# Attention and FP4 feed-forward: GpSimd sums all key tiles, ScalarE copies the first columns, two heads in one bank, TensorE's order in a pair laid anew

## The chip, the cores and the metric

One core of one Trainium2 chip. The metric is the device time of one execution in microseconds; the kernel before took 3739.86 us, the median of 3 runs (3735.11 to 3740.07).

## The reference

The input x is (8, 1024, 512). It is normalised over its last axis, and the output is x plus two branches of the normalised rows: causal attention with 16 heads of 32, and a feed-forward whose weights and activations are quantised block by block to FP4 values.

```
qkv = x @ W_attn + b_attn                       # 512 -> 1536
att = einsum('bhqd,bhkd->bhqk', q, k) * 32 ** -0.5
att = where(causal, att, -inf); att = softmax(att)
y = einsum('bhqk,bhkd->bhqd', att, v); y @ W_proj + b_proj
gate, up = fp4_linear(xn, w_gate), fp4_linear(xn, w_up)   # 512 -> 1408
fp4_linear(silu(gate) * up, w_down)
x = x + attention + feed_forward
```

The change touches only the attention.

## The kernel before, in words

The attention runs first, batch by batch, then the feed-forward over 64 tiles of 128 rows. A batch is the projections (queries, keys, values; split into high and low 32-bit parts), then 8 pairs of heads, then the output projection. Engines run side by side, each with its own program in order, and wait for each other by counting semaphores.

In a pair the scores are made twice. First with queries on the partitions: 16 tiles (`T` steps; `scores` L1020, for two heads and eight tiles of 128 queries), masked by a bf16 product (`MT`; L1046); VectorE takes each row's maximum (`row_max` L649). Tiles go by turns to ps_s and to ps_dense bank 0. These tiles are those of the next pair, 13 of the 16 ahead of the step `MAX`, the other 3 behind it for the pair after. `MAX` (L1049) transposes the maxima, VectorE splits them into high and low parts (`split_max` L656), and SP moves them by two DMAs into two extra rows of the next pair's stack (`maxima` L445). Second with keys on the partitions: for each of the eight key tiles kt 0 to 7, from query kt * 128 on, in up to 4 parts (`S0` to `S3`; `transposed_scores` L1062), the maximum subtracted by the extra rows, the diagonal masked (`M`; L1077). The parts go in a ring of three banks, ps_st; ScalarE reads each with Exp into pt, or for kt 5 to 7 into `tail` (part of rob) (L933). kt 4 takes the space of kt 1. A pair before has 24 parts: 4 each for kt 0 to 3, 2 each for kt 4 to 7.

`P0` to `P7` (`times_v` L1082) multiply the exponentials with the values. The two heads and the even and odd query tiles go to four column groups of 32 of the array. They are plain 32-bit products, two instructions each in the trace; P3, P5, P6 and P7 of a pair run at the start of the next one. `DEN` (`denominators` L1097) sums the exponentials over the keys by a product with ones, for the pair before. GpSimd has summed kt 0 to 4 in SBUF first (`sum_up` L572, into stage): kt 0 + kt 1 for queries 128 on (L583), a copy of the first 128 queries by a multiplication with ones (L580), then kt 2, 3, 4 (L585). TensorE multiplies these sums and, each for itself, kt 5, 6 and 7. In the last pair of a batch GpSimd sums kt 0 to 2 only.

VectorE copies the denominators out of the bank (`copy_den` L664), SP spreads them over 64 partitions by four DMAs (`den_rows` L488), VectorE takes reciprocals (`INV`), SP writes them out and reads them back, and VectorE divides (`Y0`, `Y1`; L690) two pairs later. The next tile in ps_dense behind DEN waits for the copy (L1035).

STEPS (L96) writes TensorE's order in a pair by hand, one string for each key tile; VECTOR_STEPS (L106) VectorE's order (`R` a row maximum). EARLY and AFTER_DEN count T steps from STEPS; DEN waits until the tiles ahead of it that use its bank have been reduced (L1101). SP's queue within a pair is: den_rows of the pair before, its inverse, the next pair's maxima, the inverse's spread, and the loads of the pair four later once this pair's exponentials are done (L507 to L525). ScalarE waits at kt 5 for den_full of the pair before (L925), since DEN reads `tail`.

Of the kernel before, what the change touches and what calls it, by code (L numbers as in the profile page):

```python
# [44 lines left out]
def attention(nc, ctx, banks, memory, shared, x, w_attn, b_attn, w_proj, b_proj, w_gate, w_up, w_down, qk_scratch, ones_scratch,  # L45
# [20 lines left out]
    PARTS = [[(h, max(c * QC, kt * P), (c + 1) * QC - max(c * QC, kt * P))  # L66
              for c in reversed(range(NQ)) if (c + 1) * QC > kt * P for h in range(2)] for kt in range(ST)]
# [13 lines left out]
    def summed(p):  # L81

        return RINGED if p < PAIRS - 1 else 3


    SUM_ORDER = [1, 0, 2, 3, 4]
    FREED = {0: 2, 1: 1, 2: 3, 3: 4, 4: 5}
    SUMS = sum(summed(p) for p in range(PAIRS))
# [7 lines left out]
    STEPS = ["T T MT P3 P5 T MT S0 S1 T S2 S3 M2 MT M3 P6 DEN P7",  # L96
# [7 lines left out]


    VECTOR_STEPS = "R R R Y0 R Y1 DEN R R R R R R R INV R R MAX R R R"  # L106
# [3 lines left out]
    AHEAD_OF_ALL = EARLY + FLAT[:FLAT.index("S0")].count("T")  # L110
# [26 lines left out]
    assert ND % 2 == 0 and (PAIRS * NPARTS) % ST_RING == 0  # L137
# [17 lines left out]
    def sem(name):  # L155
# [73 lines left out]
    summed_up = sem("a_summed_up")  # L229
# [19 lines left out]
              v_done, *stack_in, s_full, s_max, m_full, m_hi, m_lo, m_in, st_full, st_exp, pv_done, summed_up, den_full,  # L249
# [26 lines left out]
    def sums(h):  # L276
        return stage[:, h].rearrange("p a n -> p (a n)")

# [90 lines left out]
    assert len(TWOS) * 2 == TILES and AHEAD_OF_ALL == 6  # L369
# [168 lines left out]
    def gpsimd(pool):  # L538
# [25 lines left out]
        def body(b, final):  # L564
            for t in range(XR, ST):
                inv_std(b, t)

            def x_and_bias(t):
                pool.wait_ge(res_in[t % 2], ONE + b * (ST // 2) * DMA + (t // 2 + 1) * DMA)
                nc.gpsimd.tensor_tensor(res[:, t % 2], res[:, t % 2], bp[:, :], ALU.add).then_inc(o_res, 1)  # L570

            def sum_up(p, kt):  # L572

                pool.wait_ge(st_exp, ONE + b * PAIRS * NPARTS + p * NPARTS + PART0[kt + 1])
                if kt > 1:
                    pool.wait_ge(summed_up, ONE + b * SUMS + p * RINGED + kt)
                both = stage[:, :, :, :].rearrange("p h a n -> p h (a n)")
                cols = slice(kt * P, S)
                if kt == 0:
                    nc.gpsimd.tensor_tensor(both[:, :, 0:P], exps(0)[:, :, 0:P], ones[:, 0:1].unsqueeze(2).to_broadcast([P, 2, P]),  # L580
                                            ALU.mult).then_inc(summed_up, 1)
                elif kt == 1:
                    nc.gpsimd.tensor_tensor(both[:, :, cols], exps(0)[:, :, cols], exps(1), ALU.add).then_inc(summed_up, 1)  # L583
                else:
                    nc.gpsimd.tensor_tensor(both[:, :, cols], both[:, :, cols], exps(kt), ALU.add).then_inc(summed_up, 1)  # L585

            for i in range(2):
                pool.wait_ge(qk_out[i], ONE + b * (NQK // 2) * DMA + (NQK // 2) * DMA)
            for p in range(PAIRS):
                if p == PAIRS - 1 and not final:  # L590
                    inv_std(b + 1, 0, XR)
                if p:
                    pool.wait_ge(den_full, ONE + b * PAIRS + p)
                for kt in SUM_ORDER[:summed(p)]:
                    sum_up(p, kt)
            pool.wait_ge(bias_sum, 1)
            for t in range(ST):
                x_and_bias(t)
# [249 lines left out]
    def scalar(act):  # L848
# [14 lines left out]
        def body(b, final, rest):  # L863
# [50 lines left out]
            for p in range(PAIRS):  # L914
                for kt in range(ST):
                    if kt == RINGED - 1:
                        act.wait_ge(pv_done, ONE + b * PAIRS * ST + p * ST + PV_AT[1] + 1)
                        act.wait_ge(summed_up, ONE + b * SUMS + p * RINGED + FREED[1])
                    elif kt < RINGED and p:
                        last = RINGED - 1 if kt == 1 else kt  # L920
                        act.wait_ge(pv_done, ONE + b * PAIRS * ST + (p - 1) * ST + PV_AT[last] + 1)
                        act.wait_ge(summed_up, ONE + b * SUMS + (p - 1) * RINGED + FREED[last])
                    if kt == RINGED:
                        if p:
                            act.wait_ge(den_full, ONE + b * PAIRS + p)  # L925
                            act.wait_ge(pv_done, ONE + b * PAIRS * ST + p * ST)
                        else:
                            act.wait_ge(o_sum, ONE + b * ST)
                            act.wait_ge(o_out[1], ONE + b * (ST // 2) * DMA)
                    for i, (h, q, n) in enumerate(PARTS[kt]):  # L930
                        w = p * NPARTS + PART0[kt] + i
                        act.wait_ge(st_full, ONE + b * PAIRS * NPARTS + w + 1)
                        nc.scalar.activation(exps(kt)[:, h, q - kt * P:q - kt * P + n], ps_st[:, w % ST_RING, 0:n], ACT.Exp,  # L933
                                             scale=SCALE).then_inc(st_exp, 1)
                    if final and kt == PIECE_AT[p]:
                        shared.load_gate_up(act, p)
# [31 lines left out]
    def tensor(pe):  # L968
# [20 lines left out]
        def body(b, final):  # L989
# [72 lines left out]
            def transposed_scores(p, kt, i):  # L1062
                h, q, n = PARTS[kt][i]
# [3 lines left out]
                if w == ST_RING - 1:  # L1067
# [4 lines left out]
                last = nc.tensor.matmul(ps_st[:, w % ST_RING, 0:n], stack(p)[0:KM, 2 + h, kt * P:(kt + 1) * P],  # L1072
                                        stack(p)[0:KM, h, q:q + n], start=True, stop=not diagonal)
# [3 lines left out]
            def mask_transposed(p, kt, i):  # L1077
                w = p * NPARTS + PART0[kt] + i
                nc.tensor.matmul(ps_st[:, w % ST_RING, 0:P], causal[:, :], identb[:, :], start=False,  # L1079
                                 stop=True).then_inc(st_full, 1)  # L1080
# [16 lines left out]
            def denominators(p):  # L1097
                pe.wait_ge(summed_up, ONE + b * SUMS + p * RINGED + summed(p))
# [3 lines left out]
                for kt in range(summed(p) - 1, ST):  # L1102
                    for s in range(2):
                        if parity_tiles(kt, s) >= ST:
                            continue
                        for h in range(2):
                            if kt < summed(p):
                                src, cols = by_tile(sums(h))[:, s::2], slice(0, QC)
                            else:
                                src, cols = exps_of_parity(kt, h, s), y_cols(kt, s)  # L1110
                            last = nc.tensor.matmul(by_tile(den_bank(p)[y_rows(h, s), cols]), ones[:, :], src,  # L1111
                                                    start=kt < summed(p), stop=kt == ST - 2 + s)
# [533 lines left out]
```

## Time and profile before

| | us |
|---|---|
| median of 3 runs | 3739.86 |
| lowest, highest | 3735.11, 3740.07 |
| profiled execution, its own time | 3740.65 |
| its span | 3738.8 |
| TensorE busy | 3660.0 (98%) |
| VectorE busy | 2638.5 (71%) |
| ScalarE busy | 1199.3 (32%) |
| GpSimd busy | 930.6 (25%) |

The attention takes the first 2,150 us or so, where GpSimd is at work; the rest is the feed-forward. In the page's 40 slices of the span TensorE is at nine tenths or more in all but the first.

### The profile page before, as it was taken

The numbers are of one execution on the slowest core, as the hardware profiler recorded it, in microseconds if no ns is written. First come the engines' busy times: TensorE is split into PE (matmuls) and PEld (weight loads), VectorE is DVE, ScalarE is ACT, GpSimd is POOL, SyncE is SP. The second block draws the span as 40 slices with busy tenths as digits, with TensorE's granted clock in tenths as the row PEclk, the third lists the DMA queues.
The fourth block names the chain that finished last, engine by engine and source line by source line (L and its number), as shares of the span: only waits on it lengthen the run. The fifth ranks groups of instructions, "written<-read, shape, count | busy, mean of one in ns | idle before, by whom it ended". The sixth has DMA issues, their size and how long they took to land.

```text
span 3738.8 us, 63849 instructions
## 1 busy us (share of the span) xinstructions
PE 3660.0 (98%) x21836; PEld 2699.9 (72%) x21836; DVE 2638.5 (71%) x3834; ACT 1199.3 (32%) x2313; POOL 930.6 (25%) x462
## 2 busy tenths in 40 slices
PE   8999999999999999999999999999999999999999
PEld 6657657657656566566565578888888888888887
DVE  6675766766766766766766667777777777777776
ACT  2542532533523524514414412222222222222222
POOL 0560741642632724615615500000000000000000
PEclk9999999999999999999999999999999999999999
DMA  6525435335336245254256331100111110011110
GB/s 199 124 72 178 109 101 175 77 123 165 80 120 173 63 144 155 58 185 123 73 179 172 119 122 34 34 31 28 34 34 34 34 32 31 30 34 34 34 34 28
DMA packets 180526, 337.02 MB, mean 90 GB/s; under 512 B 42688, under 2 KB 50368, under 8 KB 179392
## 3 DMA queue, kind: packets, MB, share of 16 engines
q1 hardware_dynamic: 156096, 280.47, 26.5%
q10 hardware_dynamic: 24192, 53.49, 4.2%
q8 instruction: 135, 2.21, 0.3%
q14 instruction: 103, 0.84, 0.1%
HBM read 213.92 MB, written 118.43 MB: 89 GB/s over the span
## 4 chain that ended last, share of the span: by engine, by line
PE 90%; issue 2%; DMA 2%; DVE 2%; POOL 2%; ACT 1%; SPq 0%; ACTq 0%; DVEq 0%; POOLq 0%
PE f_ps L1523 26%; PE ps_dense L1016 13%; PE f_ps_o L1535 13%; PE ps_st L1072 9%; PE ps_s L1041 5%; PE ps_y L1093 4%; PE ps_dense L1180 4%; PE ps_dense L1093 3%; PE ps_dense L1111 3%; PE ps_dense L1041 2%; PE f_ps L1515 1%; PE ps_st L1079 1%; DMA stack<-mr 1%; POOL stage L585 1%; PE ps_s L1046 1%
## 5 line engine op out<-in xcount | busy, mean ns | idle before, releaser
L1523 PE MATMUL f_ps<-wgu,xqt 128*128 128x512 f32 (+1 forms) x4608 | 992.9, 373 | 1.4 <-DVE xqt L1383 1.4
L1523 PEld LDWEIGHTS f_ps<-wgu,xqt 128*128 128x128 f32 x4608 | 842.4, 188 | 123.0 <-DVE xqt L1383 1.7
L933 ACT ACTIVATE pt<-ps_st 128x512 f32<-128x512 f32 (+3 forms) x1152 | 550.4, 526 | 540.4 <-PE ps_st L1072 354.8
L653 DVE TENSOR_REDUCE mx<-ps_s 128x1 f32<-128x640 f32 (+3 forms) x512 | 523.8, 1023 | 212.2 <-PE ps_s L1046 203.1
L585 POOL TENSOR_TENSOR stage<-stage,pt 128x1536 f32<-128x1536 f32 (+2 forms) x176 | 519.1, 2950 | 15.2
L1535 PE MATMUL f_ps_o<-wd,hqt 128*128 128x512 f32 x2112 | 513.4, 396 | 0.2 <-DVE hqt L1409 0.2
L583 POOL TENSOR_TENSOR stage<-pt 128x1792 f32<-128x1792 f32 x64 | 256.5, 4009 | 882.6 <-ACT pt L933 882.6
L1535 PEld LDWEIGHTS f_ps_o<-wd,hqt 128*128 128x128 f32 x2112 | 392.6, 189 | 79.5 <-DVE hqt L1409 0.6
L1016 PE MATMUL ps_dense<-arena,wa 128*128 128x512 f32 x1536 | 384.1, 399 | 11.1 <-DVE rob L701 6.2
L1016 PEld LDWEIGHTS ps_dense<-arena,wa 128*128 128x128 f32 x1536 | 281.1, 189 | 73.7 <-issue 10.8
L653 DVE TENSOR_REDUCE mx<-ps_dense 128x1 f32<-128x128 f32 (+3 forms) x424 | 204.4, 482 | 87.5 <-PE ps_dense L1046 78.1
L1072 PE MATMUL ps_st<-stack 98*128 98x512 f32 (+3 forms) x768 | 250.1, 389 | 16.3 <-DMA stack<-mr 13.7
L1072 PE MATMUL ps_st<-arena 98*128 98x512 f32 (+3 forms) x768 | 252.4, 394 | 8.5 <-ACT pt L933 6.8
L1180 PE MATMUL ps_dense<-wp,yt 128*128 128x512 f32 x512 | 227.1, 594 | 2.1 <-DVE rob L701 2.0
L1072 PEld LDWEIGHTS ps_st<-arena 98*128 98x128 f32 x768 | 131.8, 189 | 133.3 <-ACT pt L933 101.0
L1470 ACT ACTIVATE silu<-f_ps 128x512 f32<-128x512 f32 (+1 forms) x192 | 106.8, 556 | 367.7 <-PE f_ps L1523 367.7
L1072 PEld LDWEIGHTS ps_st<-stack 98*128 98x128 f32 x768 | 132.4, 190 | 127.6 <-ACT pt L933 87.1
L899 ACT ACTIVATE stage<-ps_dense,bqk 128x512 fp32r<-128x512 f32 x128 | 87.6, 687 | 365.4 <-PE ps_dense L1016 310.0
L1465 ACT ACTIVATE ha<-ht 128x1408 f32<-128x1408 f32 x63 | 87.0, 1381 | 326.6 <-DVE ht L1306 326.6
L1402 DVE TENSOR_TENSOR h<-silu,f_ps 128x512 f32<-128x512 f32 (+1 forms) x192 | 122.6, 639 | 94.1 <-ACT silu L1470 90.6
L1016 PE MATMUL ps_dense<-wa,arena 128*128 128x512 f32 x768 | 188.1, 395 | 0.0
L1079 PE MATMUL ps_st<-identb,causal 128*128 128x128 bf16 x1024 | 183.1, 224 | 0.0
(135 smaller groups left out, 4943.1 us busy)
## 6 DMA issues: line engine op xcount, KB each, us to landing
qk_scratch<-stage SPq DMA_DIRECT2D x128, 512.0 KB, 2.8
stack<-qk_scratch SPq DMA_DIRECT2D x192, 256.0 KB
arena<-qk_scratch SPq DMA_DIRECT2D x192, 256.0 KB
xs<-in_L_attn_x SPq DMA_DIRECT2D x64, 256.0 KB, 3.6
rob<-in_L_attn_x ACTq DMA_DIRECT2D x64, 256.0 KB, 2.8
acc_scratch<-rob ACTq DMA_DIRECT2D x64, 256.0 KB, 2.2
xt<-in_L_attn_x SPq DMA_DIRECT2D x64, 256.0 KB, 2.6
at<-acc_scratch SPq DMA_DIRECT2D x64, 256.0 KB, 2.6
```

Of the source, the lines that this page charges most:

```text
L583: nc.gpsimd.tensor_tensor(both[:, :, cols], exps(0)[:, :, cols], exps(1), ALU.add).then_inc(summed_up, 1)
L585: nc.gpsimd.tensor_tensor(both[:, :, cols], both[:, :, cols], exps(kt), ALU.add).then_inc(summed_up, 1)
L653: nc.vector.tensor_reduce(mx[:, h * ST + q:h * ST + q + 1], scores_bank(p, n)[:, 0:(q + 1) * P], axis=AX.X, op=ALU.max, negate=True).then_ ...
L933: nc.scalar.activation(exps(kt)[:, h, q - kt * P:q - kt * P + n], ps_st[:, w % ST_RING, 0:n], ACT.Exp, scale=SCALE).then_inc(st_exp, 1)
L1016: last = nc.tensor.matmul(bank(*use), left(lh, k), right(rh, k), start=n == 0, stop=n == len(terms) - 1)
L1041: nc.tensor.matmul(out[:, k0:k1], qs, stack(p)[0:KS, 2 + h, k0:k1], start=True, stop=k1 < keys)
L1072: last = nc.tensor.matmul(ps_st[:, w % ST_RING, 0:n], stack(p)[0:KM, 2 + h, kt * P:(kt + 1) * P], stack(p)[0:KM, h, q:q + n], start=True, ...
L1079: nc.tensor.matmul(ps_st[:, w % ST_RING, 0:P], causal[:, :], identb[:, :], start=False, stop=True).then_inc(st_full, 1)
L1093: last = nc.tensor.matmul(by_tile(y_bank(p)[y_rows(h, s), y_cols(kt, s)]), v_head(kt, p, h), exps_of_parity(kt, h, s), start=kt == 0, stop ...
L1180: last = nc.tensor.matmul(bank("P", k), yt[:, g, t * P:(t + 1) * P], wp[:, g, :], start=g == 0, stop=g == G - 1)
L1523: last = nc.tensor.matmul(ps[:, SLOT[c], gu, 0:n].rearrange("p (j n) -> p j n", n=P), xqt[:, a, k], wgu[:, b, gu * FC + f // P:gu * FC + ( ...
L1535: last = nc.tensor.matmul(ps_o[:, :], hqt[:, a, k], wd[:, b, k], start=i == 0, stop=i == len(terms) - 1)
```

## The change

In all pairs but a batch's last GpSimd sums all eight key tiles (seven additions, kt 1 to 7); DEN is then the four products of the sums alone. The first 128 queries of kt 0 are copied into stage by ScalarE, ahead of the exponentials of kt 5, with a semaphore of its own (first_sums) for which DEN waits. For kt 6 and 7 both heads' scores go to one bank, with one mask product and one exponential; a pair has 22 parts. STEPS and VECTOR_STEPS are written anew: DEN moves from the end of the first string to the third, P3 and P5 behind the pair's first scores, MAX to the end of the fourth, and T tiles are mostly masked one by one. AHEAD_OF_ALL stays 6. Hunks that only name the semaphore or loosen an assertion, and blank lines, are left out.

```diff
@@ -63,8 +63,11 @@
-    PARTS = [[(h, max(c * QC, kt * P), (c + 1) * QC - max(c * QC, kt * P))
-              for c in reversed(range(NQ)) if (c + 1) * QC > kt * P for h in range(2)] for kt in range(ST)]
+    PAIRED = 6
+    PARTS = [[(range(h, h + 1), max(c * QC, kt * P), (c + 1) * QC - max(c * QC, kt * P))
+              for c in reversed(range(NQ)) if (c + 1) * QC > kt * P for h in range(2)] for kt in range(PAIRED)]
+    PARTS += [[(range(2), kt * P, (ST - kt) * P)] for kt in range(PAIRED, ST)]
     NPARTS = sum(len(parts) for parts in PARTS)
     PART0 = [sum(len(parts) for parts in PARTS[:kt]) for kt in range(ST + 1)]
     ST_RING, SLOTS, XR = 3, 4, 4
@@ -80,12 +83,13 @@
     def summed(p):
-        return RINGED if p < PAIRS - 1 else 3
-    SUM_ORDER = [1, 0, 2, 3, 4]
-    FREED = {0: 2, 1: 1, 2: 3, 3: 4, 4: 5}
-    SUMS = sum(summed(p) for p in range(PAIRS))
+        return ST if p < PAIRS - 1 else 3
+    SUM_ORDER = [*range(1, ST)]
+    FREED = {0: 1, 1: 1, 2: 2, 3: 3, 4: 4}
+    SUMS = sum(summed(p) - 1 for p in range(PAIRS))
     TILES = 2 * ST
     TILE = [(h, q) for h in range(2) for t in range(ST // 2) for q in (ST // 2 + t, ST // 2 - 1 - t)]
@@ -93,21 +97,22 @@
-    STEPS = ["T T MT P3 P5 T MT S0 S1 T S2 S3 M2 MT M3 P6 DEN P7",
-             "S0 S1 S2 T MT T MT M2 T S3 MT M3",
-             "S0 S1 T S2 T MT M2 P0 S3 T T MT M3 P1",
-             "S0 T T MT S1 S2 S3 M2 P2",
-             "S0 M3- M0 MAX T S1 MT M1",
-             "S0 T S1 M0 MT M1",
-             "S0 T MT M0 P4 S1",
-             "S0 S1 M1- M0 M1"]
-    VECTOR_STEPS = "R R R Y0 R Y1 DEN R R R R R R R INV R R MAX R R R"
+    STEPS = ["T MT T MT S0 S1 T P3 MT T MT S2 S3 T MT M2 M3",
+             "S0 P5 T MT T MT S1 S2 S3 M2 M3 T MT",
+             "S0 DEN P6 P7 P0 S1 T MT S2 S3 T MT M2 M3 T MT P1 T T MT",
+             "S0 S1 P2 S2 M2 S3 M3 MAX",
+             "S0 T MT M0 S1 M1",
+             "S0 T M0 MT S1 T MT M1",
+             "S0 P4 M0",
+             "S0 M0"]
+    VECTOR_STEPS = "R R R R R R R Y0 Y1 DEN R R R R R R INV MAX R R R"
     FLAT = " ".join(STEPS).split()
     EARLY = TILES - FLAT[:FLAT.index("MAX")].count("T")
-    AHEAD_OF_ALL = EARLY + FLAT[:FLAT.index("S0")].count("T")
+    AHEAD_OF_ALL = 6
     AFTER_DEN = EARLY + FLAT[:FLAT.index("DEN")].count("T")
     PV_HERE = [int(step[1:]) for u in range(ST) for step in STEPS[u].split() if step[0] == "P" and int(step[1:]) < u]
@@ -275,6 +280,9 @@
     def sums(h):
         return stage[:, h].rearrange("p a n -> p (a n)")
+    def both_sums():
+        return stage[:, :, :, :].rearrange("p h a n -> p h (a n)")
     def by_tile(a):
         return a.rearrange("p (t n) -> p t n", n=P)
@@ -573,13 +581,10 @@
                 pool.wait_ge(st_exp, ONE + b * PAIRS * NPARTS + p * NPARTS + PART0[kt + 1])
                 if kt > 1:
-                    pool.wait_ge(summed_up, ONE + b * SUMS + p * RINGED + kt)
-                both = stage[:, :, :, :].rearrange("p h a n -> p h (a n)")
+                    pool.wait_ge(summed_up, ONE + b * SUMS + p * (ST - 1) + kt - 1)
+                both = both_sums()
                 cols = slice(kt * P, S)
-                if kt == 0:
-                    nc.gpsimd.tensor_tensor(both[:, :, 0:P], exps(0)[:, :, 0:P], ones[:, 0:1].unsqueeze(2).to_broadcast([P, 2, P]),
-                                            ALU.mult).then_inc(summed_up, 1)
-                elif kt == 1:
+                if kt == 1:
                     nc.gpsimd.tensor_tensor(both[:, :, cols], exps(0)[:, :, cols], exps(1), ALU.add).then_inc(summed_up, 1)
                 else:
                     nc.gpsimd.tensor_tensor(both[:, :, cols], both[:, :, cols], exps(kt), ALU.add).then_inc(summed_up, 1)
@@ -591,7 +596,7 @@
                     inv_std(b + 1, 0, XR)
                 if p:
                     pool.wait_ge(den_full, ONE + b * PAIRS + p)
-                for kt in SUM_ORDER[:summed(p)]:
+                for kt in SUM_ORDER[:summed(p) - 1]:
                     sum_up(p, kt)
             pool.wait_ge(bias_sum, 1)
             for t in range(ST):
@@ -915,11 +920,11 @@
                 for kt in range(ST):
                     if kt == RINGED - 1:
                         act.wait_ge(pv_done, ONE + b * PAIRS * ST + p * ST + PV_AT[1] + 1)
-                        act.wait_ge(summed_up, ONE + b * SUMS + p * RINGED + FREED[1])
+                        act.wait_ge(summed_up, ONE + b * SUMS + p * (ST - 1) + FREED[1])
                     elif kt < RINGED and p:
                         last = RINGED - 1 if kt == 1 else kt
                         act.wait_ge(pv_done, ONE + b * PAIRS * ST + (p - 1) * ST + PV_AT[last] + 1)
-                        act.wait_ge(summed_up, ONE + b * SUMS + (p - 1) * RINGED + FREED[last])
+                        act.wait_ge(summed_up, ONE + b * SUMS + (p - 1) * (ST - 1) + FREED[last])
                     if kt == RINGED:
                         if p:
                             act.wait_ge(den_full, ONE + b * PAIRS + p)
@@ -927,11 +932,18 @@
                         else:
                             act.wait_ge(o_sum, ONE + b * ST)
                             act.wait_ge(o_out[1], ONE + b * (ST // 2) * DMA)
-                    for i, (h, q, n) in enumerate(PARTS[kt]):
+                            for i in range(2):
+                                act.wait_ge(qk_out[i], ONE + b * (NQK // 2) * DMA + (NQK // 2) * DMA)
+                        nc.scalar.activation(both_sums()[:, :, 0:P], exps(0)[:, :, 0:P], ACT.Copy).then_inc(first_sums, 1)
+                    for i, (heads, q, n) in enumerate(PARTS[kt]):
                         w = p * NPARTS + PART0[kt] + i
                         act.wait_ge(st_full, ONE + b * PAIRS * NPARTS + w + 1)
-                        nc.scalar.activation(exps(kt)[:, h, q - kt * P:q - kt * P + n], ps_st[:, w % ST_RING, 0:n], ACT.Exp,
-                                             scale=SCALE).then_inc(st_exp, 1)
+                        if len(heads) == 1:
+                            nc.scalar.activation(exps(kt)[:, heads[0], q - kt * P:q - kt * P + n], ps_st[:, w % ST_RING, 0:n],
+                                                 ACT.Exp, scale=SCALE).then_inc(st_exp, 1)
+                        else:
+                            nc.scalar.activation(exps(kt), ps_st[:, w % ST_RING, 0:2 * n].rearrange("p (h n) -> p h n", h=2),
+                                                 ACT.Exp, scale=SCALE).then_inc(st_exp, 1)
                     if final and kt == PIECE_AT[p]:
                         shared.load_gate_up(act, p)
@@ -1060,7 +1072,7 @@
                 last.then_inc(q_full, 1)
             def transposed_scores(p, kt, i):
-                h, q, n = PARTS[kt][i]
+                heads, q, n = PARTS[kt][i]
                 w = p * NPARTS + PART0[kt] + i
                 if (kt, i) == (0, 0):
                     pe.wait_ge(m_in, ONE + b * PAIRS * 2 * DMA + (p + 1) * 2 * DMA)
@@ -1069,15 +1081,21 @@
                     pe.wait_ge(s_max, ONE + b * PAIRS * TILES + TILES + AHEAD_OF_ALL)
                 pe.wait_ge(st_exp, ONE + b * PAIRS * NPARTS + max(w - ST_RING + 1, 0))
                 diagonal = q == kt * P
-                last = nc.tensor.matmul(ps_st[:, w % ST_RING, 0:n], stack(p)[0:KM, 2 + h, kt * P:(kt + 1) * P],
-                                        stack(p)[0:KM, h, q:q + n], start=True, stop=not diagonal)
+                for j, h in enumerate(heads):
+                    last = nc.tensor.matmul(ps_st[:, w % ST_RING, j * n:(j + 1) * n], stack(p)[0:KM, 2 + h, kt * P:(kt + 1) * P],
+                                            stack(p)[0:KM, h, q:q + n], start=j == 0, stop=not diagonal)
                 if not diagonal:
                     last.then_inc(st_full, 1)
             def mask_transposed(p, kt, i):
+                heads, _, n = PARTS[kt][i]
                 w = p * NPARTS + PART0[kt] + i
-                nc.tensor.matmul(ps_st[:, w % ST_RING, 0:P], causal[:, :], identb[:, :], start=False,
-                                 stop=True).then_inc(st_full, 1)
+                if len(heads) == 1:
+                    nc.tensor.matmul(ps_st[:, w % ST_RING, 0:P], causal[:, :], identb[:, :], start=False,
+                                     stop=True).then_inc(st_full, 1)
+                else:
+                    nc.tensor.matmul(ps_st[:, w % ST_RING, 0:2 * n].rearrange("p (h n) -> p h n", h=2)[:, :, 0:P], causal[:, :],
+                                     identb[:, :].unsqueeze(1).to_broadcast([P, 2, P]), start=False, stop=True).then_inc(st_full, 1)
             def times_v(p, kt):
@@ -1095,21 +1113,22 @@
                 last.then_inc(pv_done, 1)
             def denominators(p):
-                pe.wait_ge(summed_up, ONE + b * SUMS + p * RINGED + summed(p))
+                pe.wait_ge(summed_up, ONE + b * SUMS + p * (ST - 1) + summed(p) - 1)
+                pe.wait_ge(first_sums, ONE + b * PAIRS + p + 1)
                 if p + 2 < PAIRS:
                     pe.wait_ge(s_max, ONE + b * PAIRS * TILES + (p + 2) * TILES + AFTER_DEN // 2 * 2)
-                for kt in range(summed(p) - 1, ST):
+                for s in range(2):
+                    for h in range(2):
+                        last = nc.tensor.matmul(by_tile(den_bank(p)[y_rows(h, s)]), ones[:, :], by_tile(sums(h))[:, s::2],
+                                                start=True, stop=summed(p) == ST)
+                for kt in range(summed(p), ST):
                     for s in range(2):
                         if parity_tiles(kt, s) >= ST:
                             continue
                         for h in range(2):
-                            if kt < summed(p):
-                                src, cols = by_tile(sums(h))[:, s::2], slice(0, QC)
-                            else:
-                                src, cols = exps_of_parity(kt, h, s), y_cols(kt, s)
-                            last = nc.tensor.matmul(by_tile(den_bank(p)[y_rows(h, s), cols]), ones[:, :], src,
-                                                    start=kt < summed(p), stop=kt == ST - 2 + s)
+                            last = nc.tensor.matmul(by_tile(den_bank(p)[y_rows(h, s), y_cols(kt, s)]), ones[:, :],
+                                                    exps_of_parity(kt, h, s), start=False, stop=kt == ST - 2 + s)
                 last.then_inc(den_full, 1)
             split = 0
```

## Rows read from the trace of the kernel before

**Rows 1.** The chain that ended last: share of the span by engine and line.
```profile
PE 90%; issue 2%; DMA 2%; DVE 2%; POOL 2%; ACT 1%; SPq 0%; ACTq 0%; DVEq 0%; POOLq 0%
PE f_ps L1523 26%; PE ps_dense L1016 13%; PE f_ps_o L1535 13%; PE ps_st L1072 9%; PE ps_s L1041 5%; PE ps_y L1093 4%; PE ps_dense L1180 4%; PE ps_dense L1093 3%; PE ps_dense L1111 3%; PE ps_dense L1041 2%; PE f_ps L1515 1%; PE ps_st L1079 1%; DMA stack<-mr 1%; POOL stage L585 1%; PE ps_s L1046 1%
```

**Rows 2.** Busy time of each engine (instructions) in one pair, then granted clock and DMA.
```profile
722.10:741.70 19.60, 19.60 (x171) 12.04 (x170) 14.53 (x23) 10.60 (x25) 13.36 (x5) 1.00 0.11 26
```

**Rows 3.** TensorE in order of time, pairs 4 and 5: start, us, instructions.
```profile
715.13 0.70 PE L1072 MATMUL ps_st<-stack 98*128 98x512 f32 x2
...
717.15 1.04 PE L1111 MATMUL ps_dense<-stage,ones 128*32 128x512 f32 x8
...
725.83 0.50 PE L1072 MATMUL ps_st<-stack 98*128 98x512 f32 x1
...
726.17 0.63 PE L1041 MATMUL ps_s<-stack 96*128 96x512 f32 x2
...
730.38 0.22 PE L1079 MATMUL ps_st<-identb,causal 128*128 128x128 bf16 x1
...
730.41 0.36 PE L1072 MATMUL ps_st<-stack 98*128 98x256 f32 x1
...
730.61 0.56 PE L1041 MATMUL ps_s<-arena 96*128 96x512 f32 x2
...
736.74 1.04 PE L1111 MATMUL ps_dense<-stage,ones 128*32 128x512 f32 x8
...
737.60 1.05 PE L1111 MATMUL ps_dense<-rob,ones 128*32 128x128 f32 x20
...
738.48 0.39 PE L1093 MATMUL ps_dense<-rob,v 128*32 128x128 f32 x4
```

**Rows 4.** TensorE in order of time, the last pair of the same batch.
```profile
774.92 1.07 PE L1111 MATMUL ps_dense<-stage,ones 128*32 128x512 f32 x8 [0.47 <-POOL stage L585]
...
789.33 0.62 PE L1111 MATMUL ps_s<-stage,ones 128*32 128x512 f32 x2
...
792.65 1.53 PE L976 MATMUL ps_st<-ident,xs 128*128 128x128 f32 x12
```

**Rows 5.** Groups by line and shape, GpSimd in the attention: busy us, mean ns.
```profile
L585 POOL TENSOR_TENSOR stage<-stage,pt 128x1536 f32<-128x1536 f32 x64 | 222.6, 3478 | 5.5
...
L585 POOL TENSOR_TENSOR stage<-stage,pt 128x1280 f32<-128x1280 f32 x56 | 163.8, 2926 | 4.8
...
L585 POOL TENSOR_TENSOR stage<-stage,pt 128x1024 f32<-128x1024 f32 x56 | 132.7, 2370 | 4.8
```

**Rows 6.** GpSimd in order of time, two pairs.
```profile
726.78 8.94 POOL L585 TENSOR_TENSOR stage<-stage,pt 128x1536 f32<-128x1536 f32 x3
...
741.71 4.01 POOL L583 TENSOR_TENSOR stage<-pt 128x1792 f32<-128x1792 f32 x1 [5.99 <-ACT pt L933]
```

**Rows 7.** VectorE: three lines' durations (ns min/median/max), then its order of time.
```profile
L670 DVE COPY rob<-ps_dense x56: 691/692/694, 126.2 to 2120.9; 128x512 f32<-128x512 f32 x56
...
L615 DVE TENSOR_SCALAR xs<-xs,mv x56: 533/542/3684, 247.2 to 1904.1; 128x512 f32<-128x512 f32 x56
...
L659 DVE CAST mr<-ps_dense x56: 278/279/280, 115.3 to 2111.8; 16x128 fp32r<-16x128 f32 x56
...
776.97 0.69 DVE L670 COPY rob<-ps_dense 128x512 f32<-128x512 f32 x1 [1.78 <-PE ps_dense L1111]
...
783.05 0.25 DVE L674 RECIPROCAL inv<-den 128x16 f32<-128x16 f32 x1 [5.39 <-DMA den<-rob]
```

**Rows 8.** Start of a batch's second pair: TensorE's waits, its order of time, granted clock.
```profile
PE ps_st L1072 <- DMA stack<-mr: 13.7, 8, 4.7
...
654.86 0.86 PE L1072 MATMUL ps_st<-stack 98*128 98x512 f32 x2 [1.71 <-DMA stack<-mr]
...
658.13 1.33 PE L1111 MATMUL ps_dense<-stage,ones 128*32 128x512 f32 x8
...
657.00:658.00 1.00, 1.00 (x13) 0.56 (x15) 0.30 (x1) 0.41 (x1) 0.00 (x0) 0.50 1.08 221
```

More of the change, by code:

```diff
@@ L136, in attention @@
     assert NQ == 2 and XR == PER and AHEAD == ST - XR and len(QK) == NQK and len(PROJ) == NQK + ST + ST - XR
-    assert ND % 2 == 0 and (PAIRS * NPARTS) % ST_RING == 0
+    assert ND % 2 == 0
     F = w_gate.shape[0]
@@ L228, in attention @@
     bias_cols, bias_full, bias_sum = sem("a_bias_cols"), sem("a_bias_full"), sem("a_bias_sum")
-    summed_up = sem("a_summed_up")
+    summed_up, first_sums = sem("a_summed_up"), sem("a_first_sums")
     den_full = sem("a_den_full")
@@ L248, in attention @@
     LOOPED = [*x_in, bn_part, bn_tile, var_eps, rstd, normed, kept, d_full, t_full, t_hi, t_lo, qk_hi, qk_lo, *qk_out,
-              v_done, *stack_in, s_full, s_max, m_full, m_hi, m_lo, m_in, st_full, st_exp, pv_done, summed_up, den_full,
+              v_done, *stack_in, s_full, s_max, m_full, m_hi, m_lo, m_in, st_full, st_exp, pv_done, summed_up, first_sums, den_full,
               den_copy, den_in, inverted, last_inverted, inv_out, inv_in, y_div, *res_in, o_res, o_sum, *o_out,
@@ L368, in attention @@
         BESIDE[at] = [(1, 2 * i), (1, 2 * i + 1)]
-    assert len(TWOS) * 2 == TILES and AHEAD_OF_ALL == 6
+    assert len(TWOS) * 2 == TILES and AHEAD_OF_ALL >= EARLY + FLAT[:FLAT.index("S0")].count("T")
     NEEDS = {("QK", i): (c + 1) * PER for i, (_, _, c) in enumerate(QK)}
```

## The prediction

> **What bounds the kernel now.** I read the chain of waits first: TensorE holds 90% of it, and about 30% of the whole sits on the attention's lines (ps_st, ps_s, ps_y, ps_dense of L1041 to L1111) [rows 1]. So only what TensorE does or waits for counts. One steady pair by windows: TensorE is busy for all of its 19.6 us, VectorE 14.5, ScalarE 10.6, GpSimd 13.4 [rows 2]. The two DEN steps of rows 3 stand 736.74 - 717.15 = 19.59 us apart: that is the period of a pair, and TensorE's own work sets it.
>
> I cut a batch at its DEN steps (the order number is that of the pair whose denominators they make): A, from pair 1's first key scores to DEN(0); B, the five intervals DEN(0) to DEN(5); C, DEN(5) to DEN(6); D, DEN(6) to the end of DEN(7). Before, B's interval is 19.59; C is 774.92 - (736.74 + 19.59) = 18.59; D is 792.65 - 774.92 = 17.7 [rows 3, 4]. What comes ahead of A and behind D is the same code.
>
> **B, the steady pair.** Each term is a difference on TensorE.
> - DEN: its 20 instructions on the last three key tiles take 738.48 - 737.60 = 0.88 us [rows 3], and go. The eight on the sums stay, 0.86 us.
> - Masks: T and S tiles are masked at once now, one by one. In the old order a 32-bit product comes straight behind a mask 9 times in a pair, in the new one 20 times (counted in STEPS). Such a return costs an unhidden weight load: from the mask at 730.38 to the next scores at 730.61 are 0.23 us for 128 + 256 columns; at 0.42 ns a column (DEN: 4 x 512 columns, an estimate, in 0.86) that is 0.16, so 0.07 is left [rows 3]. 11 x 0.07 = +0.77. The bounds: 0, and the 0.13 that 512 columns have over their 0.21 behind a times-V step (725.83 to 726.17) [rows 3], so 0 to 1.4; I take the row of the same kind, a mask.
> - Leaving times-V steps: 6 exits into 32-bit products become 4, two go into a mask: about -0.1; five of the six times-V groups are now entered from a 32-bit product rather than a mask, no row of that; -0.5 to +0.2, I take -0.2. Fewer short products back to back: -0.15. One mask over two heads instead of two, twice a pair: -0.03.
> - Short waits in the old order (the tile behind DEN on VectorE's copy, two on its maxima), some 0.1 each: -0.3, if the new order has none.
> Sum: -0.88 + 0.77 - 0.1 - 0.2 - 0.15 - 0.03 - 0.3 = -0.9. Pair 18.7 us, B = -4.5 a batch.
>
> Does a wait come instead? GpSimd: sums of key tiles 1 to 4 take 4.01 [rows 6] + 3.48 + 2.93 + 2.37 [rows 5]; each 256 elements less are 0.53 to 0.56 less, so 5, 6, 7 take an estimated 1.81, 1.26, 0.70. With six gaps of 0.065 (three L585 as one block take 8.94 [rows 6] against 8.78 by the means) that is 16.95 us. It now runs DEN to DEN: the first sum waits for den_full, DEN for the last sum. 16.95 + 0.86 + 0.2 of entry + 0.17 of two releases (0.05 was seen behind POOL at 774.92) = 18.2. That is 0.5 us under 18.7: no wait, but the floor. Before, it ended its block at 735.72 and then sat 6.0 us until the exponentials of key tile 1 [rows 6].
> ScalarE: two exponentials saved, one copy of 256 columns added; with 10.6 of 19.6 busy [rows 2] both hide, at worst 0.4 us of it is seen. VectorE: before DEN it reduces seven tiles and divides twice; by laying the steps out with those durations I get the reduction that DEN needs 0.1 to 0.2 us ahead, the division that P0 needs 0.2 ahead: thin, up to +0.3 if they miss. The inverse chain: copy to reciprocal took 783.05 - 777.66 = 5.4 us where the DMA was waited for [rows 7]; copy to INV are six reductions, about 5.7 us, and behind INV on SP's queue stand the inverse's DMA, then the maxima's. Their landing has some 1.5 us to spare before the next pair's first key scores. In ahead of these there are 4.7 us of TensorE work from MAX instead of 6.2, as P3 and P5 stand behind them now.
>
> **A, the start.** Pair 1's first scores wait for the maxima's DMA, which lies behind pair 2's and 3's loads: 13.7 us over 8 batches, 4.7 the longest [rows 8]. The DMA lands when it did; TensorE is there 1.5 us sooner, so the hole grows from 1 to 1.7 us (most batches) to 2.5 to 3.2, and the work comes behind it. From the first scores to DEN were 717.15 - 715.13 = 2.0 us [rows 3]. Now there are 9 key-score products and 6 tiles (7,680 columns, 3.2 us), 10 masks (0.6), P3 and P5 (1.07 + 0.5 of entries and exits), 8 returns (0.6): 6.1. A = +4.1.
> **C.** Pair 6 has no tiles behind MAX, pair 7 none: TensorE would be at DEN(6) 15.5 us behind DEN(5) (2.0 + 10.6 for the rest of pair 6, less DEN's, and pair 7's nine key scores at ScalarE's speed), GpSimd's cycle says 18.2. C = 18.2 - 18.6 = -0.4, with a hole of about 2.6 us ahead of DEN(6).
> **D.** Kt 0 and 1 of pair 7 are ahead of DEN now. Behind DEN(6): DEN 1.05, P6 P7 0.43, P0 0.85, P1 and P2 2.0 with entries, key scores of tiles 2 to 7 with masks and returns 3.9, P4 0.65, P3 P5 P6 P7 1.8, DEN(7) as before 792.65 - 789.33 = 3.3 [rows 4], ring waits 0.3: 14.3. D = -3.4. VectorE's chain (copy, 5.4 of DMA, norms, divide) ends just then and has the projections' start for cover, as before.
> **The clock.** Behind the 1.71 us hole [rows 8] the granted clock was 0.50, the lower of its two levels; first scores to DEN took 658.13 - 654.86 = 3.3 instead of 2.0, and some 0.3 more was lost after. So a fall costs about 1.6 us. The other holes before are shorter, most near 1 to 1.5 us, and not each was followed by a fall (an estimate: two or three of eight). Two longer holes a batch: I count 1.4 falls more a batch, +2.2; bounds 0 and 3.2.
>
> **The sum.** A +4.1, B -4.5, C -0.4, D -3.4, clock +2.2: -2.0 us a batch, -16 for 8. The profiled execution took 3740.65 us (span 3738.8, 1.9 around it), 0.8 over the median of 3739.86 and no more than 0.6 over the highest: 3740.7 - 16 = 3725, against the median 3724.
>
> **A rule against the change.** SBUF — State Buffer, section "Who interferes with whom", of the Trainium skill: VectorE and GpSimd share a pair of ports under an exclusive lock; copies and tensor_scalar can want it, the loser waits for the other's whole instruction. Rows first: L615, a tensor_scalar SBUF to SBUF, has 542 ns as median and 3684 as its most, beside a GpSimd add of 3.5 us; L670, the copy of the denominators out of PSUM, has 691 to 694 in all 56, but GpSimd stood still by it; now its 4 us add starts at the same moment. The cast L659, also out of PSUM, has 278 to 280 always, and GpSimd ran beside it [rows 7]. The trace agrees with the rule for L615, and speaks against its reach to sources in PSUM.
>
> **Rivals.**
> 1. GpSimd becomes the bound: returns cost less than 0.03, and the pair stands at 18.2. For it: its cycle is just 0.5 below. Against: the count of returns. B = -6.9; 3724 - 19 = 3705, and 3688 if the clock never falls. Chance 0.2.
> 2. Slower: the alternation of masks and scores in u0 to u2 costs 0.13 or more a return, the upper row. The pair gains 0.25, B = -1.2, a batch +1.3 or more, and with three falls' worth of clock +2.3: 3750 (3745 to 3758). It decides once a pair gains under 0.5, from 0.11 a return: A's and the holes' +2.5 are then no longer paid. For it: 20 against 9. Against: the 0.07 measured behind masks. Chance 0.14.
> 3. Level: gain and holes cancel (a pair gains 0.4 to 0.6, or P0 and DEN wait their 0.3 for VectorE): 3738. Chance 0.2. TensorE: Matmul & The Clock Gate, section "LDWEIGHTS", of the Trainium skill puts a load of 128 columns at an estimated 107 ns; unhidden in all 11 new returns the pair would gain 0.5 and the time stay at 3740. The rows show 70 ns left over behind a mask, so I weigh it no more than that.
> 4. The copy waits for GpSimd's 4.0 us add [rows 6]: the tile behind DEN waits, less the 1.8 us of P6, P7, P0, S1 ahead of it: +2.9 a pair after its gain, in 56 pairs some 3870. Chance 0.02.
> 5. That it doesn't do what it says (exponentials of tiles 6 and 7 in two banks still): excluded by the code.
>
> **Chances.** The forecast has 0.44, 3724, with its own range of 3708 to 3736 (B by 0.3 us a pair either way, 12 us, and the clock). What a measurement of this kernel can tell is 0.2%, 7.5 us. Faster: 0.42 of the forecast and 0.2 of rival 1. Same: rival 3 and 0.02 of the forecast, less 0.02 of its edges: 0.21. Slower: 0.14 + 0.02, 0.01 more from rival 3's edge: 0.17. The range, 3690 to 3748, reaches to rival 1 and into rival 2.
>
> **What would show it.** DEN to DEN 18.7 us in pairs 1 to 5; at 18.2 with TensorE's L1111 waiting for POOL in each, rival 1; over 19.1, rival 2, by gaps behind masks. L1111 with 8 instructions a pair and none from rob, GpSimd with seven ops back to back. A hole ahead of pair 1's first scores of 2.5 to 3.2 us, one ahead of DEN(6) of 2 to 4, granted clock 0.5 behind both. DEN(6) to DEN(7)'s end 14.3 to 16. Wrong would be: no holes, a wait at P0 or at the tile behind DEN in each pair, L670 over 0.7 us.

## The result, and the profile after

The changed kernel took 3748.30 us (median of 20 runs, 3738.02 to 3759.94); the kernel before, 3739.87 (20 runs). The ratio is 1.0026, 95% interval 1.0018 to 1.0034: slower, by about 9 us, where 16 less was forecast. The profiled execution took 3741.61, one of its quickest.

Page of the changed kernel: span, TensorE's busy time, its granted clock by slices.
```profile
span 3739.8 us, 61509 instructions
...
PE 3629.0 (97%) x20588; PEld 2610.8 (70%) x20588; DVE 2618.2 (70%) x3834; ACT 1190.2 (32%) x2249; POOL 1109.5 (30%) x566
...
PEclk9999999999999999999999999999999999999999
```
TensorE is busy 31 us less than before in the same span. The slices are too coarse for the reason: the mean granted clock of the run is 0.987, before 0.996. In windows of 1 us through the attention I added up what is missing to 1.00: 8.5 us in 4 falls before, 42.6 us in 17 falls after. (A fall here is a stretch in which the granted clock is at 0.50; half of its length is lost clock.) The other runs agree: the quickest (3738.0) had a clock of 0.987, the slowest (3759.9) 0.981; 0.006 of 3,750 us are 22. The median run has 0.985.

A steady pair, windows as in [rows 2].
```profile
717.99:736.59 18.60, 18.60 (x150) 10.28 (x148) 14.29 (x23) 10.36 (x23) 16.62 (x8) 1.00 0.25 56
```
The pair takes 18.60 us; 18.7 was forecast. But not every pair does: DEN steps lie 18.61, 19.21, 18.63, 18.61 and 19.59 us apart in this batch.

TensorE's waits in the attention (us in total, times, longest), as in [rows 8].
```profile
PE ps_st L1085 <- DMA stack<-mr: 29.7, 8, 7.0
PE ps_dense L1123 <- POOL stage L590: 17.1, 8, 2.5
...
PE ps_st L1085 <- DMA arena<-mr: 6.6, 15, 0.9
```
The first row was 13.7, the second 3.8; the third is new: the waits for the maxima in pairs 3, 6 and 7.

The two holes of one batch on TensorE, answering to [rows 8] and [rows 4]: first key scores of pair 1, DEN(0); the last scores ahead of DEN(6), DEN(6), DEN(7).
```profile
654.37 1.22 PE L1085 MATMUL ps_st<-stack 98*128 98x512 f32 x2 [3.14 <-DMA stack<-mr]
...
663.12 1.07 PE L1123 MATMUL ps_dense<-stage,ones 128*32 128x512 f32 x8
...
773.63 0.50 PE L1085 MATMUL ps_st<-arena 98*128 98x512 f32 x1
776.16 1.93 PE L1123 MATMUL ps_dense<-stage,ones 128*32 128x512 f32 x8 [2.03 <-POOL stage L590]
...
787.89 0.62 PE L1123 MATMUL ps_s<-stage,ones 128*32 128x512 f32 x2
```
Their windows: us, TensorE busy, ..., granted clock (third from the end).
```profile
652.00:660.00 8.00, 5.63 (x22) 2.91 (x22) 2.20 (x4) 1.23 (x3) 5.16 (x4) 0.57 0.89 200
653.00:659.00 6.00, 4.63 (x17) 2.26 (x18) 0.84 (x2) 1.09 (x2) 4.16 (x4) 0.50 1.00 219
775.00:779.00 4.00, 2.83 (x24) 1.35 (x28) 0.69 (x1) 0.05 (x1) 2.93 (x5) 0.59 0.02 4
776.00:779.00 3.00, 2.83 (x24) 1.35 (x28) 0.69 (x1) 0.00 (x0) 2.01 (x4) 0.50 0.03 5
```
In this batch the holes have the length that was forecast (2.5 to 3.2, 2 to 4). Over all eight, the first is 2.7 to 3.5 us, 7.0 in the last batch, and the one ahead of DEN(6) 1.8 to 2.5. In this batch the clock then sits at 0.50, the lower level, for 6.8 us at the first hole and 3.4 at the second. DEN's eight instructions take 1.9 us at 776.16, against 1.07.

GpSimd, answering to [rows 6], and the copy of the denominators.
```profile
759.02 4.00 POOL L588 TENSOR_TENSOR stage<-pt 128x1792 f32<-128x1792 f32 x1 [2.47 <-PE ps_dense L1123]
763.10 8.95 POOL L590 TENSOR_TENSOR stage<-stage,pt 128x1536 f32<-128x1536 f32 x3
772.13 3.98 POOL L590 TENSOR_TENSOR stage<-stage,rob 128x768 f32<-128x768 f32 x3
```
```profile
L675 DVE COPY rob<-ps_dense x56: 690/692/693, 132.1 to 2123.6; 128x512 f32<-128x512 f32 x56
```
The three new sums take 3.98 us (3.77 was the estimate, without the gaps between them); the copy is not held up by the add beside it (rival 4 falls).

### The profile page after: what moved, and what is told of

It reads as the page before. It is cut to its first block, busy times and chain, and to the rows that moved or that the text cites. A ratio compares the mean times of both kernels' runs of the same rounds, so it can differ in the third digit from the quotient of the medians.

```text
span 3739.8 us, 61509 instructions
## 1 busy us (share of the span) xinstructions
PE 3629.0 (97%) x20588; PEld 2610.8 (70%) x20588; DVE 2618.2 (70%) x3834; ACT 1190.2 (32%) x2249; POOL 1109.5 (30%) x566
## 4 chain that ended last, share of the span: by engine, by line
PE 89%; DMA 3%; issue 3%; DVE 2%; POOL 1%; ACT 1%; SPq 1%; ACTq 0%; DVEq 0%; POOLq 0%
PE f_ps L1542 26%; PE ps_dense L1028 13%; PE f_ps_o L1554 13%; PE ps_st L1085 7%; PE ps_s L1053 5%; PE ps_dense L1199 5%; PE ps_y L1111 4%; PE ps_dense L1111 4%; PE ps_dense L1123 2%; PE ps_dense L1053 1%; DMA stack<-mr 1%; PE f_ps L1534 1%; DMA arena<-mr 1%; POOL stage L590 1%; PE ps_st L1094 1%
## 5 line engine op out<-in xcount | busy, mean ns | idle before, releaser
L942 ACT ACTIVATE pt<-ps_st 128x512 f32<-128x512 f32 (+3 forms) x1152 | 537.9, 526 | 570.2 <-PE ps_st L1085 398.8
L1085 PE MATMUL ps_st<-stack 98*128 98x512 f32 (+3 forms) x768 | 260.4, 405 | 30.0 <-DMA stack<-mr 29.7
L1085 PE MATMUL ps_st<-arena 98*128 98x512 f32 (+3 forms) x768 | 254.9, 402 | 10.2 <-DMA arena<-mr 6.6
L590 POOL TENSOR_TENSOR stage<-stage,rob 128x768 f32<-128x768 f32 x168 | 215.5, 1283 | 14.6
```

The source lines that it names most:

```text
L942: nc.scalar.activation(exps(kt)[:, heads[0], q - kt * P:q - kt * P + n], ps_st[:, w % ST_RING, 0:n], ACT.Exp, scale=SCALE).then_inc(st_exp, 1)
L1085: last = nc.tensor.matmul(ps_st[:, w % ST_RING, j * n:(j + 1) * n], stack(p)[0:KM, 2 + h, kt * P:(kt + 1) * P], stack(p)[0:KM, h, q:q + n] ...
```

## The experiments

Theory: the steps are worth about what was forecast, and the clock falls behind the two holes take it back. Times are medians, each with its ratio to the kernel before on the same chip; the changed kernel stands at 1.0026. The chips differ a little, so a difference between two versions can come out some 3 us apart by times and by ratios.

**e1: TensorE kept busy in both holes.**
```diff
+                    if p == 1:
+                        filler(12)      # 128x512 bf16 products into ps_y, ahead of the wait for m_in
...
+                if p == PAIRS - 2:
+                    pe.wait_ge(y_div, ONE + b * PAIRS * 2 + (PAIRS - 2) * 2)
+                    filler(9)           # ahead of the wait for summed_up
```


> The changed kernel with idle TensorE time filled: twelve bf16 products of 512 columns into a free bank ahead of the wait for the maxima in each batch's second pair, nine ahead of the wait for GpSimd at DEN(6). They change no value and shorten no wait. Theory (the clock falls behind the two longer holes are the term I mis-sized): granted clock back from 0.987 to about 0.995, one or two falls in the attention instead of 17, and 22 to 34 us less than the changed kernel, 3714 to 3726. Rival 1 (the falls are absorbed by later waits, the loss is in the order of the steps): within 4 us of the changed kernel. Rival 2 (fillers lengthen the holes): slower by up to 5 us.

3710.45, ratio 0.9919 (0.9906 to 0.9932): 38 us less than the changed kernel (40 by the ratios; 22 to 34 was expected), by work that does nothing. Two falls are left, both in the last batch, 8.5 us of lost clock. The batch from above:
```profile
644.65 2.75 PE L1076 MATMUL ps_y<-identb,causal 128*128 128x512 bf16 x12
648.14 0.73 PE L1092 MATMUL ps_st<-stack 98*128 98x512 f32 x2 [0.74 <-DMA stack<-mr]
...
654.53 1.06 PE L1133 MATMUL ps_dense<-stage,ones 128*32 128x512 f32 x8
...
766.59 1.07 PE L1133 MATMUL ps_dense<-stage,ones 128*32 128x512 f32 x8 [0.30 <-POOL stage L590]
...
776.89 0.62 PE L1133 MATMUL ps_s<-stage,ones 128*32 128x512 f32 x2
```
Scores to DEN(0) take 6.4 us instead of 8.75, DEN(6) to DEN(7) 10.3 instead of 11.7. The waits themselves are no shorter: 2.75 us of filler and 0.74 of idle time stand where 3.14 us of idle time stood. The theory stands.

**e12: the same filler in the kernel before** (five products, first hole only).

> The kernel before with five bf16 products of 512 columns ahead of the wait for the maxima in each batch's second pair, to have it without clock falls too. It had four falls in the attention, 8.5 us of lost clock, not all of it under work. Theory: 3732 to 3737, so that the change without the clock is worth 3710 against some 3735, and the clock is why it was not seen. Rival (fillers give more than the clock, as they also shift the work): under 3725.

3737.70, ratio 0.9998 (0.9989 to 1.0007): no difference. The run can't say what a fall costs, though: of the four falls before, this filler takes away two (1.7 us of lost clock each, near 655 and 1188 us), the two of the last batch stay, and its interval is 3 to 4 us wide on either side. What it gives is the comparison without the added falls: 3710 against 3738, 27 us (30 by the ratios). The forecast without its clock term is 4.2 us a batch, 34 us. So the steps are worth a little less than was forecast, and most of the miss is the clock.

**e2: pair 3's loads behind pair 1's maxima.**
```diff
-            later = stack_loads(2) + stack_loads(3)
+            later = stack_loads(2)
...
                     maxima(p + 1)
+                if p == 0:
+                    for args in stack_loads(3):
+                        load(*args)
```


> The changed kernel with the seven loads of pair 3's stack issued behind the maxima of pair 1 on SP's queue, not before pair 0. Theory (the maxima's DMA queues behind 3 MB of loads, so the hole ahead of pair 1's first scores is DMA backlog): the wait for stack<-mr falls from 29.7 us to under 12 us in total, no clock fall behind it, 20 to 30 us less than the changed kernel. Rival (the landing is set by when MAX comes, or by the loads of pair 4 issued behind): wait stays over 24 us, time within 5 us of the changed kernel.

3707.96, ratio 0.9911 (0.9897 to 0.9925), 40 us less (20 to 30 was expected). The wait for stack<-mr is gone. From issue to landing, the two DMAs of pair 1's maxima take, in the batch from above, in the changed kernel and then here:
```profile
DMA to landing us min/median/max: 5.1/5.6/6.2
DMA to landing us min/median/max: 1.8/1.8/1.8
```
So the first hole is a small DMA behind or beside the stack loads. Some comes back as waits for GpSimd and the split maxima (DEN(0) to DEN(1) 19.9 instead of 18.6, and 26.7 instead of 18.8 in the last batch); 11 falls are left, 7 of them at DEN(6).

**e6: the same edit in the kernel before.**

> The kernel before with the seven loads of pair 3's stack behind the maxima of pair 1. It had the hole ahead of pair 1's first scores too, but 1.3 us shorter, and four clock falls. Theory: stack<-mr waits 13.7 to under 5 us, 3724 to 3732. Rival (only the changed kernel's order suffers from these loads): 3737 to 3742.

A miss: 3764.18, ratio 1.0061 (1.0047 to 1.0074), slower by 22. VectorE in pair 1:
```profile
669.87 0.41 DVE L656 TENSOR_REDUCE mx<-ps_dense 128x1 f32<-128x256 f32 x1
673.51 0.25 DVE L677 RECIPROCAL inv<-den 128x16 f32<-128x16 f32 x1 [3.23 <-DMA den<-rob]
```
The loads now run beside the DMAs of the denominators. Those of pair 1 in this batch, from issue to landing, in the kernel before and then here:
```profile
DMA to landing us min/median/max: 1.7/1.7/1.7
DMA to landing us min/median/max: 7.2/7.7/7.9
```
INV waits for them in VectorE's order, ahead of the last maxima, and TensorE waits for those: DEN(0) to DEN(1) takes 21.5 to 30 us instead of 19.6 to 20.2. In the changed kernel DEN(0) comes some 4 us of work later, and the same DMAs take 5.2 us in e2. The same wait was only moved.

**e4: five of the eight sums in pair 6.**
```diff
-        return ST if p < PAIRS - 1 else 3
+        return ST if p < PAIRS - 2 else 5 if p == PAIRS - 2 else 3
```
(and running offsets for summed_up)

> The changed kernel with GpSimd summing only kt 1 to 4 of a batch's last-but-one pair; DEN(6) multiplies kt 5 to 7 itself, as before the change (0.88 us more TensorE work in 8 pairs). Theory (DEN(6) waits for GpSimd, 17.1 us in 8 batches, and the clock falls behind it): that wait goes to 0, no fall at the batch's end, 15 to 22 us less than the changed kernel. Rival (ScalarE or the inverse chain bounds the last pair anyway): the wait reappears within the last pair, 0 to 5 us.

3726.51, ratio 0.9963 (0.9949 to 0.9978): 22 us less. DEN(5) to DEN(6) takes 16.1 to 16.6 us instead of 18.4, no wait for GpSimd, no fall behind it.

**e5: e2 and e4 together.**

> The changed kernel with both holes shortened: pair 3's loads behind pair 1's maxima, and GpSimd summing only kt 1 to 4 of a batch's last-but-one pair. Theory (each hole costs its length and a clock fall behind it, the two are independent): 3708 less some 14 to 20 us: 3688 to 3696, under 5 falls in the attention. Rival (with one hole gone the other's cost moves on into a new wait for GpSimd or VectorE): 3700 to 3708.

3688.19, ratio 0.9859 (0.9844 to 0.9874): 52 us less than the kernel before, the best version here. The two repairs nearly add.

**e3: P3 and P5 ahead of the first key scores again.**
```diff
-    STEPS = ["T MT T MT S0 S1 T P3 MT T MT S2 S3 T MT M2 M3",
-             "S0 P5 T MT T MT S1 S2 S3 M2 M3 T MT",
+    STEPS = ["T MT P3 P5 T MT S0 S1 T MT T MT S2 S3 T MT M2 M3",
+             "S0 T MT T MT S1 S2 S3 M2 M3 T MT",
```


> The changed kernel with P3 and P5 put back ahead of the pair's first key scores; all else as it is. Theory (the hole grew because 1.2 us of work was moved behind the wait): stack<-mr waits fall from 29.7 by 8 x 1.2 us to about 20, the waits for arena<-mr in steady pairs (6.6 us) vanish, intervals of 19.1 to 19.6 us between DEN steps go to 18.6; 12 to 25 us less than the changed kernel, the larger figure if clock falls go with them. Rival (P3 and P5 ahead only shift the wait to the scores' ring or to VectorE): within 5 us.

A miss: 3766.37, ratio 1.0066 (1.0054 to 1.0078), 18 us slower. Its waits, same view as above:
```profile
PE ps_s L1053 <- DVE mx L658: 36.5, 88, 5.0
PE ps_st L1085 <- DMA stack<-mr: 19.3, 8, 5.7
```
The hole shrank as expected (29.7 to 19.3), but VectorE runs dry while P3 and P5 run, then tiles wait for it: 19.58 us in nearly every pair. VectorE in one of them:
```profile
724.42 1.09 DVE L658 TENSOR_REDUCE mx<-ps_s 128x1 f32<-128x896 f32 x1 [1.33 <-PE ps_s L1058]
```
The clock is worse too: 58 us lost in the attention of the profiled execution, where the changed kernel lost 42.6, although the holes are shorter. Ahead of pair 1's first scores they are 1.6 to 2.2 us in seven batches, and the falls behind them last 6.8 or 10.2 us. A shorter hole did not make a shorter fall.

**e9, e10: smaller moves of that kind, on e5** (P3 alone ahead; or a third tile ahead).

> The version with both holes shortened (3688), with P3 alone put ahead of the pair's first key scores (P5 stays behind). Pairs 3 and 6 still lose 0.6 us each to the wait for the maxima, and pair 7 some. Theory (0.8 us of cover ends that wait, and VectorE has enough tiles to bridge P3): 18.6 in all intervals from DEN(1) on, 3676 to 3684. Rival (as when P3 and P5 both went ahead: VectorE runs dry and tiles wait for it): 19 us or more in every pair, 3700 to 3730.

> The same version (3688) with three tiles ahead of the first key scores instead of two, P3 behind them. 0.17 us of cover, and VectorE is fed sooner. Theory: the wait in pairs 3 and 6 shrinks by 0.2 us, 3683 to 3688. Rival (the third tile waits for VectorE and delays the key scores, ScalarE starves): 3690 to 3710.

3704.34 (0.9908; 0.9893 to 0.9923) and 3694.57 (0.9883; 0.9868 to 0.9898), both slower than e5: 19.4 and 19.06 us in most pairs, where e5 has 18.6 in some and 19.2 in others. Both rivals were right.

**e11: masks together, on e1** ("T T MT" for "T MT T MT" in the first string, and behind P5).

> The filled changed kernel (3710) with two mask steps merged into the next: the first two tiles of a pair and the first two behind P5 are masked together, so that two returns of a 32-bit product behind a mask go. By my prediction's term that is 2 x 0.07 us in 56 pairs, 8 us less: 3701 to 3706. Rival (the first mask of the two comes 0.4 us later, and VectorE with its 0.8 us a tile waits for it, so tiles wait later): 3715 to 3740, VectorE's waits longer.

3725.30 (0.9967; 0.9955 to 0.9979), 15 us slower than e1 (18 by the ratios), where my term for returns gave 8 less. VectorE of e11:
```profile
729.40 0.56 DVE L658 TENSOR_REDUCE mx<-ps_dense 128x1 f32<-128x384 f32 x1 [1.12 <-PE ps_s L1058]
```
It starts that tile 1.12 us after its last work, in e1 0.72 after. The pair takes 19.17 us instead of 18.6.

**e7: the old order of steps with the new sums and banks, filled.** DEN alone is moved, behind the first scores of kt 2.

> The changed kernel's sums, banks and fillers, but TensorE's old order of steps, with DEN alone moved behind the first key scores of kt 2 and VectorE's order of the changed kernel. It asks what the new order itself is worth, to be compared with 3710 for the filled kernel. By my prediction (each of 11 returns behind a mask costs 0.07 us, the old order has them not) TensorE's own work is 0.5 us less a pair, and GpSimd's cycle of 18.4 bounds it: 18.4 a pair, 3700 to 3708. Rival (the order feeds VectorE evenly, and the old one lets TensorE wait for maxima or for the copy of the denominators): 19 us a pair or more, 3722 to 3745.

A miss, beyond both ranges: 3762.71 (1.0058; 1.0044 to 1.0072), 52 us slower than e1. Its steady pair is 19.8 to 19.96 us. The waits of one:
```profile
PEld ps_st L1091 <- ACT pt L941: 3.6, 6, 0.8
...
PEld ps_dense L1132 <- DVE mx L657: 1.5, 2, 0.8
```
DEN waits 0.46 us for a maximum, and scores wait in groups for ScalarE's ring. VectorE's order is the new one here, so this bounds the worth of the new order rather than measures it.

**e8: kt 6 and 7 in two banks again, filled.**

> The filled kernel with key tiles 6 and 7 as before: a bank, a mask and an exponential for each head (24 parts a pair). It asks what the pairing is worth, against 3710. By my prediction 0.03 us of TensorE a pair, hidden on ScalarE: 3709 to 3714. Rival (ring slots and ScalarE's extra 0.34 us a pair delay the scores behind them): 3718 to 3730.

A miss: 3768.02 (1.0073; 1.0059 to 1.0086), 58 us slower than e1; a pair is 19.53. TensorE, then ScalarE, at the pair's end:
```profile
736.53 0.31 PE L1092 MATMUL ps_st<-stack 98*128 98x128 f32 x1
737.14 0.33 PE L1092 MATMUL ps_st<-stack 98*128 98x128 f32 x1 [0.30 <-ACT rob L942]
```
```profile
734.70 0.42 ACT L937 ACTIVATE stage<-pt 128x256 f32<-128x256 f32 x1
735.00 0.89 ACT L942 ACTIVATE rob<-ps_st 128x384 f32<-128x384 f32 x2
736.70 0.66 ACT L942 ACTIVATE rob<-ps_st 128x256 f32<-128x256 f32 x2 [0.81 <-PE ps_st L1101]
```
The parts of kt 6 and 7 need a bank that ScalarE has still to empty, and its new copy (0.42) stands just ahead. From the exponentials of kt 5 to those of the next pair are 3.75 us, in e1 2.83. The copy is in both versions, so this run prices the pairing, not the copy; no run leaves the copy out.

Not all of the 58 us are the pairing. Three falls came at DEN(6) here, of 10.2, 3.4 and 10.2 us, in batches 2, 4 and 6 (counted from 0), and ahead of none of them is a hole. Windows ahead of the first and in it:
```profile
764.70:776.70 12.00, 11.37 (x94) 5.78 (x85) 9.19 (x23) 6.17 (x18) 11.08 (x4) 1.00 0.12 20
777.00:786.00 9.00, 9.00 (x34) 3.54 (x34) 1.38 (x2) 4.39 (x9) 6.40 (x6) 0.50 0.01 3
```
TensorE was busy for 11.4 of the 12 us and idle for at most 0.3 at a time, and the clock fell all the same.

## Why the prediction was wrong

- **A, the start:** +4.1 without the clock. e1 has 6.4 us from first scores to DEN(0), I had 6.1 (its terms add up to 6.0); the hole of 3.14 was in my range, those of other batches up to 0.3 us over it. Right.
- **B, the pair:** 18.7 forecast, 18.6 found, but only in three of five intervals. The other two are 18.8 to 19.7: the maxima's DMA lands up to 0.9 us too late in pairs 3 and 6 (and 0.2 in pair 7). I gave it "some 1.5 us to spare". The two DMAs of pair 3's maxima in the batch from above, from issue to landing, in the kernel before and after:
```profile
DMA to landing us min/median/max: 1.8/1.8/1.8
DMA to landing us min/median/max: 1.8/2.6/3.4
```
The second of them lands 3.1 to 3.9 us after its issue in pairs 3 and 6 of seven batches. What holds it up there I have not examined. B was 1.0 us a batch too good, 0.2 once the clock is held up (e1).
- **B's parts:** the sum held, its parts did not. "One mask over two heads instead of two: -0.03" is -0.9 by e8: I priced it by TensorE's own time, and its worth is that the bank comes free sooner. Whether it pays for ScalarE's copy, which I had hidden by its share of busy time, is argued and not shown. The term of +0.77 for returns behind masks has no support: merging two of them costs 0.57 (e11), as each tile feeds VectorE at once. With TensorE's old order and VectorE's new one, the new sums are slower than the kernel before (e7). What a return costs by itself stays open.
- **C, D:** DEN(5) to DEN(6) 18.4, I had 18.2; from DEN(6) to DEN(7)'s start 10.3 us in e1, I had 11.0. Right. In GpSimd's cycle the six gaps should have been 0.08 us each by [rows 6], not 0.065.
- **The clock, the step that failed:** "I count 1.4 falls more a batch, +2.2; bounds 0 and 3.2". Found are 13 falls more (1.6 a batch), so the count was nearly right, but 34 us of lost clock, 4.3 a batch, beyond my bound; e1 gives 38 us back in the medians. The term that failed is the price of a fall: I took 1.6 us from one example, a fall of 3.4 us, and found 34 / 13 = 2.6. Six of the 17 falls last 6.8 us or more, one of them 13.7. In the median run the clock is 0.985 against 0.996 in e1, 0.011 of 3,750 us, so it lost still more than the profiled one.
- **The sum again:** in the mean of the first seven batches, A, B, C and D changed by +4.3, -4.1, -0.3 and -4.0 us from e12 to e1, both without falls there: -4.1, where I had -4.2. From the kernel before to the changed kernel they changed by +6.3, -3.5, -0.2 and -2.6: 0.0, where I had -2.0. Most of the difference sits in A and D, right behind the two holes.
- **Rivals:** 1 and 4 are refuted (TensorE waits for GpSimd once a batch; the copy takes 692 ns). 2 has the measured time (3750) but not the reason: a pair gains 0.7 us on average, not 0.25, and the holes and the clock make the kernel slower. 3 (level) has the profiled execution's time, but not its conditions: a pair gains more than the 0.6 it names, and I find no wait of TensorE for VectorE at P0 or at DEN. Rival 4's own sum doesn't come out either: 56 times 2.9 us are 162, not the 130 to 3870.

What sets the length of a fall stays open. In the changed kernel five of the six long ones stand behind a hole of over 3 us, but behind holes of 3.4, 3.4 and 3.5 us the fall was 3.4; e3 has long falls behind short holes, and e8 has falls behind none.

## What to carry to other kernels

Where a tuned pipeline gets shorter in its steady part, look at its ends first: a fixed latency that was covered now stands open, and an idle TensorE costs its idle time once and the lower clock behind it again. A filler that does nothing separates the two in one run. Price such a loss from many examples, or give it a wide bound: one example was too low by more than a third here. And price a change to shared banks by when a bank comes free, not by the work of one engine: the pairing of two heads, which saves TensorE 0.03 us by my count, was worth 0.9 a pair.

## What the runs showed of the hardware

Falls of the granted clock to 0.50 came behind idle stretches of TensorE of 1.8 to 7.0 us in the changed kernel, of 1.5 to 4.8 us in the kernel before, and three times in e8 behind a stretch with no idle time over 0.3 us at once. Single falls cost from 1.7 to 6.8 us of lost clock in the changed kernel: one example is no price. The DMAs of pair 1's denominators landed 1.7 us after their issue in the kernel before and 7.7 us beside stack loads (e6); those of its maxima 5.6 us with the loads of pair 3 issued ahead of them and 1.8 us with these behind (e2).
